# Seven entries of a hand-written step table moved by one step, in a fused attention kernel on one core

## The reference

```python
x_norm = modulate(_ln(x), shift_a, scale_a)
q, k, v = split(x_norm @ W_qkv + b_qkv)              # 16 heads of 8 channels
x = x + gate_a * (softmax(q k^T * scale) v @ W_proj + b_proj)
q_c = _ln(x) @ W_qc + b_qc;  k_c, v_c = split(_ln(context) @ W_kvc + b_kvc)
x = x + (softmax(q_c k_c^T * scale) v_c @ W_cproj + b_cproj)
x = x + gate_m * (gelu(modulate(_ln(x), shift_m, scale_m) @ W_mlp1 + b_mlp1) @ W_mlp2 + b_mlp2)
```

## Time and profile before

| what | us |
|---|---|
| median of the runs | 570.68 |
| lowest and highest of 3 runs | 568.03, 572.41 |
| span of the profiled execution | 569.2 |
| of it TensorE busy | 536.2 |
| VectorE, ScalarE, GpSimd busy | 433.4, 384.8, 276.2 |

### The profile page before, as it was taken

The page is one execution under the profiler, slowest core; times in us unless marked ns, Lnnn a source line. Parts: engine busy times, 40 slices in busy tenths (PEclk is TensorE's granted clock), DMA queues, the critical chain, the costliest instruction groups (busy, mean ns, idle before and its releaser), DMA issues.

```text
span 569.2 us, 16513 instructions
## 1 busy us (share of the span) xinstructions
PE 536.2 (94%) x6209; PEld 388.2 (68%) x6209; DVE 433.4 (76%) x1271; ACT 384.8 (68%) x897; POOL 276.2 (49%) x296
## 2 busy tenths in 40 slices
PE   6988999899999999999999889998999999999995
PEld 5745666566656666666667566655888788788895
DVE  4778889788989889898877577865586686786565
ACT  6536778687777787877877575564764864864862
POOL 5637849579497787888840422224224124124100
PEclk9989999899999999999999899999999999999999
DMA  4765635534154352453410010000000000000000
GB/s 131 159 172 132 178 101 159 123 95 112 51 133 119 96 134 68 113 134 82 125 32 5 1 37 1 1 1 18 20 20 20 28 24 24 19 20 18 18 20 18
DMA packets 48716, 39.38 MB, mean 69 GB/s; under 512 B 6241, under 2 KB 48002, under 8 KB 48642
## 3 DMA queue, kind: packets, MB, share of 16 engines
q1 hardware_dynamic: 46568, 34.62, 23.2%
q10 hardware_dynamic: 2074, 3.77, 2.4%
HBM read 10.06 MB, written 2.10 MB: 21 GB/s over the span
## 4 chain that ended last, share of the span: by engine, by line
PE 64%; DVE 13%; POOL 7%; DMA 5%; issue 4%; ACT 4%; SPq 2%; ACTq 0%; DVEq 0%; POOLq 0%
PE PS L959 31%; PE PS L1837 7%; PE PS L1803 6%; PE PS L1889 4%; PE PS L995 3%; PE PS L1901 3%; DMA Qs<-MT 2%; PE PS L1821 2%; DVE NM L1617 2%; PE PS L1859 2%; PE PS L1894 2%; SPq L1347 2%; DVE r_T L934 2%; DVE r_R L937 1%; PE PS L1881 1%
## 5 line engine op out<-in xcount | busy, mean ns | idle before, releaser
L1617 DVE TENSOR_REDUCE NM<-PS 128x4 f32<-128x512 f32 x256 | 163.3, 681 | 30.1 <-PE PS L1803 29.5
L1503 ACT ACTIVATE PR<-PS 128x512 f32<-128x512 f32 x256 | 139.7, 599 | 27.2 <-PE PS L1821 26.6
L1803 PEld LDWEIGHTS PS<-Ks,Qs 64*128 64x128 bf16 x1024 | 57.7, 95 | 53.8 <-DVE NM L1617 29.6
L1803 PE MATMUL PS<-Ks,Qs 64*128 64x128 bf16 x1024 | 83.8, 219 | 5.2 <-DVE NM L1617 3.8
L1821 PE MATMUL PS<-Qs,Ks 64*128 64x128 bf16 x1024 | 84.2, 220 | 4.1 <-DMA Qs<-MT 3.5
L1837 PE MATMUL PS<-PR,Va 128*32 128x128 f32 x2048 | 84.2, 283 | 0.0
L742 ACT ACTIVATE r_HID<-PS,ANC 128x128 f32<-128x128 f32 x224 | 63.0, 381 | 19.4 <-PE PS L959 19.4
L653 POOL TENSOR_TENSOR m_veps<-m_mv,m_eps 128x4 f32<-128x4 f32 x16 | 3.6, 224 | 132.6 <-DVE m_mv L821 132.6
L1837 PEld LDWEIGHTS PS<-PR,Va 128*32 128x32 f32 x2048 | 49.0, 110 | 20.9 <-ACT PR L1503 6.5
L1821 PEld LDWEIGHTS PS<-Qs,Ks 64*128 64x128 bf16 x1024 | 57.5, 95 | 7.9 <-DMA Qs<-MT 4.0
L959 PE MATMUL PS<-r_NXS,r_WNS 128*128 128x512 f32 x168 | 53.2, 424 | 0.0
(11 more groups left out here) (201 smaller groups left out, 1121.2 us busy)
## 6 DMA issues: line engine op xcount, KB each, us to landing
Qs<-Qp SPq DMA_DIRECT2D x96, 128.0 KB
Ks<-Kp SPq DMA_DIRECT2D x90, 128.0 KB
CTXG<-in_ctx SPq DMA_DIRECT2D x8, 256.0 KB, 3.8
r_CTX<-in_ctx SPq DMA_DIRECT2D x8, 256.0 KB, 2.8
out<-X SPq DMA_DIRECT2D x8, 256.0 KB, 2.3
X<-in_x SPq DMA_DIRECT2D x7, 256.0 KB, 4.3
W<-in_weights ACTq DMA_DIRECT2D x2, 855.0 KB
Qs<-MT SPq DMA_DIRECT2D x62, 8.0 KB
```

The costliest lines, as they stand in the source:

```text
L1503: nc.scalar.activation(PR[:, u, :], T_BANK[u % 2][:, :], ACT.Exp, scale=SCALE)\
L1617: nc.vector.tensor_reduce(out=NM[:, c.b // 2, c.second, u // 2, u % 2 * 4:u % 2 * 4 + 4, 0], in_=S_BANK[score_bank(c, u)[0]][:, :].rearran ...
L1803: last = nc.tensor.matmul(S_BANK[bank][:, j * P:(j + 1) * P], Qs[c.stack][rows, lo + j, cols], Ks[c.stack][rows, lo + j, cols], start=True ...
```

## The change

In `regular_steps` four fills, with their reads, get a time later by one step: `q0` from 4.0 to 5.0, `yt_c` from 12.0 to 13.0, `q1` from 20.0 to 21.0 and `v0` from 23.0 to 24.0. In `crossed_steps` the two `xt_x` and `yt_c` likewise. Nothing else is changed.

```diff
-            + fill_steps(4.0, "q0", i + 1, (0, 4.1), (1, 4.2))
+            + fill_steps(5.0, "q0", i + 1, (0, 5.1), (1, 5.2))
...
-            + fill_steps(12.0, "yt_c", i - 3, (1, 12.1))
+            + fill_steps(13.0, "yt_c", i - 3, (1, 13.1))
...
-            + fill_steps(20.0, "q1", i + 1, (0, 20.1), (1, 20.2))
-            + fill_steps(23.0, "v0", i + 1, (1, 23.1))
+            + fill_steps(21.0, "q1", i + 1, (0, 21.1), (1, 21.2))
+            + fill_steps(24.0, "v0", i + 1, (1, 24.1))
...
-            + fill_steps(4.0, "xt_x", g, (1, 4.1)) + fill_steps(6.0, "q0", i + 1, (0, 6.1), (1, 6.2))
+            + fill_steps(5.0, "xt_x", g, (1, 5.1)) + fill_steps(6.0, "q0", i + 1, (0, 6.1), (1, 6.2))
...
-            + fill_steps(10.0, "proj_c", i - 3, (1, 10.1)) + fill_steps(12.0, "yt_c", i - 3, (1, 12.1))
+            + fill_steps(10.0, "proj_c", i - 3, (1, 10.1)) + fill_steps(13.0, "yt_c", i - 3, (1, 13.1))
...
-            + fill_steps(20.0, "xt_x", g + 1, (1, 20.1)) + fill_steps(22.0, "q1", i + 1, (0, 22.1), (1, 22.2))
+            + fill_steps(21.0, "xt_x", g + 1, (1, 21.1)) + fill_steps(22.0, "q1", i + 1, (0, 22.1), (1, 22.2))
```

## The result

| | before | after |
|---|---|---|
| median of the runs, us | 569.97 | 575.82 |
| lowest and highest, us | 568.03, 572.41 | 574.67, 576.92 |
| span of the profiled execution, us | 569.2 | 575.1 |

Four runs of each stand behind the medians. By them the change makes the kernel 5.85 us slower, where 6.5 was forecast; the ratio is 1.0112, with a 95% interval of 1.0078 to 1.0147. Now and then an execution of any of these kernels is much slower than the rest; the ratios leave such runs out, and they can differ by up to 0.3% from the quotient of the medians that stand beside them. The profiled execution of after took 576.92 us, 1.8 more than its span.

A forecast was written before the change was run, and what follows sets the result against it. TensorE sets the pace, VectorE and ScalarE close behind. `q0` 3.1, `q1`/`v0` 0.7, `yt_c` 1.9, crossed 1.1, round 0 0.5, less 0.8 given back: +6.5 on 570.7, 577.2 us; own range 574 to 580, 8 in 10 within 570.5 to 581.5.

The forecast's parts named there:

- Given back: Rounds 1 and 2: 0.8 us less, returned by waits for stacks and maxima that end with a DMA.
- `q0` to `k0`, each of rounds 1 to 4: Scores of steps 4 and 5 wait for exponentials, then `k0` for the read of `q0`: +0.77 us a round.
- `q1` and `v0`, each round: Scores of steps 20 and 21 wait for exponentials, +0.38; `v0` behind the turn back gains 0.20: together +0.18 us.
- `xt_c`, round 3, at its place: `xt_c` waits for VectorE's read of `yt_c`, behind maxima and normalization: +2.02 us, 1.11 after two later waits absorb some.
- `xt_c`, round 4: Same wait for VectorE's read of `yt_c`, without `ln_s` statistics: +0.76 us, no later wait absorbs it.
- crossed rounds 5 and 6: Projections behind `xt_x` wait for its read, four times; VectorE takes some back: between 0.6 and 1.6, taken as +1.1 us.
- rounds 0 and 1 as a whole: Round 0 was put at 0.5 us, bounded by 0 and 0.77; round 1 has the regular `q0`, `q1` and `v0` costs.
- The single move: Crossed rounds: each of four `xt_x` moves delays the next projection, `q0` or `q1`, by 0.40 us.
- The cheaper fills decide: Rival: not slower; 4.4 us saved on fills and 0.17 before `q0` in four rounds, 565.6 us; chance 0.05.
- Half taken back: Rival: delays are real, but VectorE and ScalarE get ahead and later waits shrink; +3, 573.7 us; chance 0.35.
- No saving behind a turn: Rival: weights are not loaded during the turn, so moved fills cost what they did; 581.6 us; chance 0.04.
- GpSimd's order decides: Rival: `q1` split 1.2 us later, K and Q stacks behind it, next round's step 2 waits; 582.0 us; chance 0.05.

The follow-up runs named there:

- `v0` alone: Kernel before with only the `v0` fill moved, from 23.0 to 24.0; 568.47 us against 568.75, ratio 0.9997.
- `q1` alone: Kernel before with only the `q1` fill moved, from 20.0 to 21.0; 567.6 us against 569.09, ratio 0.9982.
- statistics alone: Kernel before with only the second part of GpSimd's `ln_x` statistics moved, from 3.2 to 5.3; 567.9 us against 569.09, ratio 0.9973.
- all edits together: Kernel before with `k0`, `xt_c`, `v0`, crossed `q0`, `q1`, `yt_c` behind turns and `ln_x` statistics at 5.3; 565.29 us against 569.09, ratio 0.9912.
- the one with the read of `xt_s` later: Kernel after with ScalarE's second read of `xt_s` in regular rounds at 4.1 instead of 2.1; 574.72 us against 569.16 before, ratio 1.0073.
- `q0` back: Kernel after with `q0` of the regular rounds back at 4.0; 573.65 us against 568.75 before, ratio 1.0083.
- the kernel with the next fills moved: Kernel before with `k0` at 5.0, `xt_c` 13.0, `v0` 24.0, crossed `q0` 5.0 and `q1` 21.0; 569.55 us against 568.75, ratio 1.0017.

## Why the prediction was right, step by step

The table sets the terms of the sum beside the trace. "Given back" of rounds 1 and 2 is split evenly over the two.

| term | forecast, us | trace, us |
|---|---|---|
| `q0` to `k0`, each of rounds 1 to 4 | +0.77 | +0.82, 0.82, 0.82, 0.81 |
| `q1` and `v0`, each round | +0.18 | +0.24, 0.22, 0.22 (rounds 2 to 4) |
| `xt_c`, round 3, at its place | +2.02 | +2.03 |
| of it left behind the two waits | +1.11 | +0.99 |
| `xt_c`, round 4 | +0.76 | +0.82 |
| round 2 as a whole | +0.55 | +0.52 |
| crossed rounds 5 and 6 | +1.1 | +1.84 |
| rounds 0 and 1 as a whole | +1.05 | -0.65 |

**The steps that held.** `q0`: from the end of the exponentials to the start of `k0` the forecast had 2.64 us (187.46 to 190.10); it is 192.04 - 189.36 = 2.68. Each link was read from a row of before: signal and half a block, turn 0.50, fill 0.95, 0.11 to the read, 0.69 for it, 0.05 to `k0`. `yt_c`: VectorE's order, walked through instruction by instruction, gave a read that frees `xt_c` 2.79 late, and the waits of 0.23 and 0.68 behind it used up. Counted from the start of the round, `xt_c` is 2.85 late in the trace, 0.82 of it from `q0`, and both waits are gone. By the distances between blocks these two are 0.30 and 0.74, more than the brackets show; taken off 2.03 they leave the 0.99 of the table. That ScalarE's backlog causes 0.57 of the wait at step 4 is shown by moving its read alone (0.97 to 0.40). The prediction named the exponentials only; VectorE's maxima, which hold the scores for the 0.40 that is left, are not in it, and in the kernel after they are hidden behind the exponentials.

**The terms that were mis-sized.** The crossed rounds: 1.84 in the profiled execution, above the range of 0.6 to 1.6. Part of that is chance. Round 5 holds a wait for the Q stack that differs from run to run; over the four kernels whose crossed rounds are those of before (before, `v0` alone, `q1` alone, statistics alone) round 5 lasts 36.49, 36.85, 36.69 and 36.88, and over the six that have them as after 37.69, 37.41, 37.54, 37.22, 37.73 and 37.53. The means differ by 0.79, and with the 0.63 of round 6 the term is 1.4. The single move was sized well (0.40 against 0.43 and 0.44 in round 6); what VectorE takes back between the places was set too high (0.5), and the crossed `yt_c`, costed at nothing, gains 0.23 a round.

Rounds 0 and 1: +1.05 forecast, -0.65 found. The execution profiled before had a granted clock of 0.87 from 28 to 42 us and 0.96 in round 1; the one after had 1.00 in both stretches. Over all profiles here round 0 ends anywhere from 69.85 to 75.11 us and round 1 lasts from 36.67 to 38.95, whatever the kernel. The forecast term is neither borne out nor refuted. So the sum is near partly by luck: one term too low stands beside one that the profile shows lower; rounds 2 to 6 alone were forecast at 5.4 and measured at 6.24 and 5.95.

**The rivals.** "The cheaper fills decide" failed at the point it named: a read needs 0.85 and the values behind the fill last 0.57. "Half taken back" failed: rounds 2 to 6 keep all of it but the two waits of round 3 and that of round 2 for the K stack, which the sum had counted. "No saving behind a turn" failed: turn 0.49 and projection 0.95 in the kernel after, and 0.99 for `v0` behind the turn back, where it took 1.09. The Trainium skill, page "TensorE: Matmul & The Clock Gate", section "The mechanism", has weight loads overlap only matmuls in flight of other row groups. By that sentence nothing would be saved behind a full-array turn; these slots differ from that, as does the weight load that starts at 190.13 under the turn, and the measurement decides. (The same section also lets a load into the background weight buffer go ahead of matmuls in flight; whether this is such a load no run here shows.) What allows this load was not tested: turn and fill have the same shape in the rows (128*128), the scores and values beside them have another (64*128, 128*32). "GpSimd's order decides" failed: no new wait at step 2 of a round, with `q1` alone or in the kernel after.

## What to carry to other kernels

Where all fills share one bank, the resource is the distance from a fill to the next one, and an earlier or cheaper fill is worth something only if its reader keeps its time: move the fill that follows, not the one whose reader is waited for. Before a piece of work is moved, ask what it covered; here a projection hid a wait of one microsecond, behind one helper's backlog and then another's, and a place in VectorE's order cost ten times what the fill saved. If such a move brings nothing, look for the bound just behind it before giving it up: the earlier fills gained nothing until GpSimd's order brought the K stack forward, and then all edits together gave 0.9% (0.6 to 1.2). And look in the trace whether an edit moved what it was to move: the same edit to GpSimd's order, made alone, left the split of K where it was.

## What the runs showed that was not expected

After the same wait in front of `xt_c` in round 3 (1.71 us in all four rows) the granted clock stayed at 1.00 in three executions (the two of the kernel after, and the one with the read of `xt_s` later) and fell to 0.50 in one (`q0` back), at 1.56 us for the blocks that followed. In that one the clock was still at 1.00 for more than a microsecond after TensorE was at work again (162.1 to 163.5), and at 0.50 from 164 to 167. A wait of this size was thus once followed by a loss nearly as long as itself; what decides it was not found.

SP's issue of a stack's DMA, 0.6 us as a rule, takes up to 2 us now and then, at places that change from run to run. SP's timeline in round 4 of the kernel with the next fills moved:

```profile
190.53 2.56 SPq L1347 DMA_DIRECT2D Qs<-Qp  x2
193.14 1.25 SPq L1347 DMA_DIRECT2D Ks<-Kp  x2
...
195.66 2.52 SPq L1347 DMA_DIRECT2D Ks<-Kp  x4
```

Two issues take 2.56 us in the first row and 1.25 in the second. What SP issues behind them comes later: the last issue of the K stack ends at 198.18, 19.35 us after the start of the round, in the kernel before 18.66. But this does not make the whole wait of 1.71 us. In round 2 of the same kernel that issue ends later still, 19.58 us after the start of the round, and the wait is 0.34. There the scores start 1.83 us after the end of the issue, in round 4 it takes 2.65. Why the stack landed later in that one place is open.
